# The first loads of a fused condition-and-FFN kernel in runs of 4096 bytes, and what moves with them

## The chip, the cores and the metric

One core of one Trainium2 chip. The metric is the device time of one execution in microseconds, the median of several runs. TensorE (PE) multiplies and transposes, VectorE (DVE), ScalarE (ACT) and GpSimd (POOL) work element by element, SyncE (SP) and ACT issue the transfers (DMA).

## The reference

x has 64 batches of 64 tokens of 512 columns, all float32. A condition q scales it, then comes an FFN with two of six low-rank experts:

```python
q_emb = relu(q @ W3 + b3)
v_sum = sum(v, axis=1, keepdims=True)
x1 = (n * v + v_sum) * q_emb[:, None, :]
y = relu(x1 @ W2 + b2)
base_out = y @ W_base + b_base
shared_out = (y @ A_s) @ B_s
gates = softmax(y @ W_router + b_router)       # two largest kept, others 0: w_per_e
routed_out = sum over e of ((y @ A_r[e]) * w_per_e) @ B_r[e]
out = x + base_out + shared_out + routed_out
```

## The kernel before

The 4096 tokens are worked in eight groups of 512. A group's x lies in `x_nat` by tokens (four tiles t of 128) and, turned, in four chunks c of 128 columns of x with all 512 tokens beside each other. Every product is done in three: each operand is split into a rounded part (`_hi`, made by ACT) and its rest (`_lo`, made by DVE for activations and by POOL for weights), and hi*hi, lo*hi and hi*lo are added up in a PSUM bank. The steps of a group are m1 (x1 times W2, 48 matmuls of 512 columns), h (the experts' first factors), m2 (times W_base) and up (the second factors). Groups 0 to 3 go singly, 4 to 7 in pairs. Each engine runs a program that is written out by hand in one order; semaphores join them, so an instruction that waits holds all behind it on its engine.

The change is about the beginning, group 0. SP issues (L393 to L399) the four tiles of x, the two halves of W3, the four chunks of W2 and W_base. PE first multiplies idle data (`keep_warm`), transposes the condition, then transposes x tile by tile, as each lands, into four banks `head_ps`; tile t stands in columns 128 t to 128 t + 127 of every bank, so the bank's columns are tokens in order and a batch is 64 neighbouring columns. Then it makes q in four chunks (`q`, two halves k of W3 each; float32 operands take two passes each). DVE works on a chunk in the bank itself: `sum_head` (sum per batch, then n times x plus sum), `scale_head` (times q) and, when ACT has rounded (`x1_split_head`), `rest_head`. ACT rounds W2 chunk by chunk (`W2_split`), and POOL makes the rests of W2, then of the router weights and of W_base. `m1_first` on PE consumes chunk 0, then 1, then for output tiles 0 and 1 chunks 2 and 3, then both again for tiles 2 and 3; its waits name the chunk's rounded parts and rests:

```python
for k in range(KC // 2, KC):
    pe.wait_ge(x1_hi_ready, k + 1)
    pe.wait_ge(W2_lo_ready, k + 1)
    for m in tiles:
        chunk(m, k, W2_hi, x_hi)
        chunk(m, k, W2_lo, x_hi)
        pe.wait_ge(x1_lo_ready, k + 1)
        last = chunk(m, k, W2_hi, x_lo)
```

Of the kernel before, what the change touches and what calls it, by code (L numbers as in the profile page):

```python
# [22 lines left out]
def adaln_ffn(nc, x, cond, W3, b3, W2, b2, W_base, b_base, A_s, B_s, A_r, B_r, W_router, b_router, out):  # L23
# [25 lines left out]
    WARM_LOAD, WARM_W3, WARM_HALF, WARM_Q = 8, 1, 2, 1  # L49
# [14 lines left out]
    out_groups = out.rearrange("b n d -> (b n) d").rearrange("(g t p) d -> g p t d", t=TT, p=P)  # L64

    ctx = ExitStack()
    with ctx:
# [79 lines left out]
        hT = bank("hT")  # L147
        q_ps = m1_ps
# [28 lines left out]
        vsum_head_ready = sem("vsum_head_ready")  # L177
# [209 lines left out]
        def _(sp):  # L387
# [22 lines left out]
            def store(g):  # L410

                order = list(up_order[g])
                for t in range(TT):
                    sp.wait_ge(out_ready, TT * g + 1 + max(order.index(i) for i in range(t + 1)))
                    sp.dma_start(out_groups[g][:, t, :], x_nat[g % 2][:, t, :]).then_inc(stored[g % 2], 16)
# [55 lines left out]
        def _(pool):  # L471
# [18 lines left out]
            def scale(g, c):  # L490

                pool.wait_ge(x1_sum_ready, KC * g + c + 1)
                scaled(xs[g % 2][:, c, :], g, c).then_inc(x1_full_ready, 1)
# [149 lines left out]
        def _(act):  # L643
# [8 lines left out]
            def x1_split(g, c):  # L652

                act.wait_ge(x1_full_ready, KC * g + c + 1)
# [24 lines left out]
            def W2_split(c):  # L679

                act.wait_ge(W2_loaded[c], 16)
                nc.scalar.activation(W2_hi[:, c, :], W2_f[:, c, :], ACT.Copy).then_inc(W2_hi_ready, 1)  # L682

            def x1_split_head(c):

                act.wait_ge(x1_full_ready, c + 1)
                nc.scalar.activation(x_hi[:, c, :], head_ps[c][:, :], ACT.Copy).then_inc(x1_hi_ready, 1)  # L687
# [198 lines left out]
        def _(dve):  # L886
# [41 lines left out]

            def sum_head(c):

                dve.wait_ge(head_turned, c + 1)
                nc.vector.tensor_reduce(vsum_head[:, c, :], per_batch(head_ps[c][:, :]), AX.X,
                                        ALU.add).then_inc(vsum_head_ready, 1)
                dve.wait_ge(vsum_head_ready, c + 1)
                nc.vector.scalar_tensor_tensor(
                    out=per_batch(head_ps[c][:, :]), in0=per_batch(head_ps[c][:, :]), scalar=float(N),
                    in1=vsum_head[:, c, :].unsqueeze(2).to_broadcast([P, BG, N]),
                    op0=ALU.mult, op1=ALU.add).then_inc(x1_sum_ready, 1)

            def scale_head(c):  # L940

                dve.wait_ge(qT_ready, c + 1)
                dve.wait_ge(x1_sum_ready, c + 1)
                nc.vector.tensor_tensor(per_batch(head_ps[c][:, :]), per_batch(head_ps[c][:, :]),
                                        qT[:, c, 0:BG].unsqueeze(2).to_broadcast([P, BG, N]),
                                        ALU.mult).then_inc(x1_full_ready, 1)

            def rest_head(c):

                dve.wait_ge(x1_hi_ready, c + 1)  # L950
# [77 lines left out]
            def add_x(g, *places):  # L1028

                for n in places:  # L1030
                    t = up_order[g][n]
                    if g == 0:
                        dve.wait_ge(head_loaded[t], 16)
# [293 lines left out]
        def _(pe):  # L1327
# [9 lines left out]
            nc.tensor.transpose(m1_ps[0][:, 0:B + KC], cond_sb[:, 0:P], ident[0:B + KC, 0:B + KC])  # L1337
            last = nc.tensor.transpose(m1_ps[0][:, cond_cols(1)], cond_sb[0:B, P:2 * P], ident[0:B, 0:B])
            last.then_inc(condT_done, 1)

            for t in range(TT):
                pe.wait_ge(head_loaded[t], 16)
# [15 lines left out]
            def m1(g, m):  # L1358
# [8 lines left out]
                elif m == 0 and g == PAIRED - 1:  # L1367
                    pe.wait_ge(x1_sum_ready, KC * (g + 1))
# [18 lines left out]
            def m1_first():  # L1387

                def chunk(m, k, W, x1):
                    return nc.tensor.matmul(m1_ps[m][:, :], W[:, k, m * P:(m + 1) * P], x1[:, k, :],  # L1390
                                            start=k == 0 and W is W2_hi and x1 is x_hi,
                                            stop=k == KC - 1 and x1 is x_lo)
# [26 lines left out]
                for tiles in ((0, 1), (2, 3)):  # L1419
                    for k in range(KC // 2, KC):  # L1420
                        pe.wait_ge(x1_hi_ready, k + 1)
# [220 lines left out]
```

## Time and profile before

| | us |
|---|---|
| median of 3 runs | 230.55 (230.02 to 230.58) |
| the profiled execution | 230.53 |
| its span in the trace | 228.8 |
| PE busy in the span | 224.0 (98%) |
| DVE busy | 176.1 (77%) |
| ACT busy | 110.2 (48%) |
| POOL busy | 107.0 (47%) |

The profile is one execution. Times in the trace count from the span's start; the 1.7 us between span and execution lie outside it.

### The profile page before, as it was taken

The page shows a single profiled execution, that of the slowest core. Times are in us where ns is not written, and L with a number is a line of the kernel's source. Part 1 is how long each engine was busy: PE and PEld are TensorE (multiplying, and loading weights), DVE is VectorE, ACT ScalarE, POOL GpSimd, SP SyncE. Part 2 cuts the span into 40 slices and gives each one's busy share as a digit, 9 for nine tenths or more (in the row PEclk, how much of TensorE's full clock was granted, in tenths as well). Part 3 has the DMA queues.
Part 4 walks back from the last instruction along what each step waited for, and adds up shares of the span by engine and source line. Part 5 has one row for each costly group of instructions (what it writes and reads, how often), then busy time and mean ns, then how long its engine had stood idle before and what let it go on. Part 6 is the DMA issues. An engine that isn't in the chain of part 4 may idle for free.

```text
span 228.8 us, 2915 instructions
## 1 busy us (share of the span) xinstructions
PE 224.0 (98%) x982; PEld 183.1 (80%) x982; DVE 176.1 (77%) x323; ACT 110.2 (48%) x230; POOL 107.0 (47%) x99
## 2 busy tenths in 40 slices
PE   7999999999999999999999999999999999999994
PEld 3987888888888888888888888888888788888883
DVE  0595979899979979699758899999996969382334
ACT  3178631545426345779326496344676375331010
POOL 4079444058125865889887201349988700000000
PEclk9999999999999999999999999999999999999999
DMA  6999902704049495004429844111213742002044
GB/s 194 324 240 230 276 27 53 165 3 185 10 122 261 181 229 171 15 0 182 181 39 222 150 181 141 48 19 17 82 47 127 287 148 84 0 15 47 27 165 183
DMA packets 32917, 29.05 MB, mean 127 GB/s; under 512 B 5841, under 2 KB 23317, under 8 KB 32902
## 3 DMA queue, kind: packets, MB, share of 16 engines
q1 hardware_dynamic: 31090, 28.69, 44.0%
q10 hardware_dynamic: 1812, 0.17, 0.6%
q8 instruction: 8, 0.13, 0.3%
q14 instruction: 7, 0.06, 0.1%
HBM read 18.89 MB, written 8.39 MB: 119 GB/s over the span
## 4 chain that ended last, share of the span: by engine, by line
PE 94%; DMA 2%; DVE 1%; ACT 1%; SPq 1%; issue 0%; DVEq 0%
PE m_ps L1354 77%; PE hT L1354 11%; PE m_ps L1390 5%; DMA x_nat<-in_x_dram 2%; DVE x_nat L1037 1%; PE m_ps L1382 1%; SPq L394 1%; PE m_ps L1331 0%; PE m_ps L1344 0%; ACT qT L676 0%; ACT W_hi L682 0%; ACT x_hi L687 0%; PE hT L1344 0%; DVEq L1036 0%
## 5 line engine op out<-in xcount | busy, mean ns | idle before, releaser
L487 POOL TENSOR_TENSOR xs<-xs,qT 128x512 f32<-128x512 f32 x22 | 24.1, 1096 | 46.7 <-DVE xs L911 30.8
L1354 PE MATMUL m_ps<-Wb_lo,y_hi 128*128 128x512 f32 x116 | 45.1, 389 | 0.0
L1354 PE MATMUL m_ps<-Wb_hi,y_hi 128*128 128x512 f32 x116 | 45.1, 389 | 0.0
L1354 PE MATMUL m_ps<-Wb_hi,y_lo 128*128 128x512 f32 x116 | 45.1, 389 | 0.0
L659 ACT ACTIVATE y_hi<-m_ps,condT 128x512 fp32r<-128x512 f32 x30 | 20.7, 692 | 17.5 <-PE m_ps L1354 10.0
L1354 PEld LDWEIGHTS m_ps<-Wb_hi,y_hi 128*128 128x128 f32 x116 | 21.8, 188 | 4.5
L1354 PEld LDWEIGHTS m_ps<-Wb_hi,y_lo 128*128 128x128 f32 x116 | 21.8, 188 | 4.5
L1354 PEld LDWEIGHTS m_ps<-Wb_lo,y_hi 128*128 128x128 f32 x116 | 21.8, 188 | 4.5
L926 DVE TENSOR_TENSOR y_lo<-m_ps,y_hi 128x512 fp32r<-128x512 f32 x30 | 20.2, 678 | 5.4 <-ACT m_ps L660 5.4
L1354 PE MATMUL m_ps<-x_hi,W_hi 128*128 128x512 f32 x61 | 23.7, 389 | 0.0
L1354 PE MATMUL m_ps<-x_hi,W_lo 128*128 128x512 f32 x61 | 23.7, 389 | 0.0
L1037 DVE TENSOR_TENSOR x_nat<-m_ps,x_nat 128x512 f32<-128x512 f32 x29 | 18.9, 682 | 4.6 <-PE m_ps L1354 4.6
L1354 PE MATMUL m_ps<-x_lo,W_hi 128*128 128x512 f32 x61 | 21.9, 389 | 0.0
L752 ACT ACTIVATE xs<-xs,offset,q 128x64 f32<-128x64 f32 x48 | 16.6, 431 | 8.3 <-DVE offset L305 6.9
L569 POOL TENSOR_TENSOR x_lo_more<-xs,x_hi_more 128x512 fp32r<-128x512 f32 x12 | 15.4, 1303 | 10.5 <-ACT x_hi_more L743 10.5
L660 ACT ACTIVATE m_ps<-m_ps,condT 128x512 f32<-128x512 f32 x30 | 19.9, 664 | 0.0
L1057 DVE STREAM_TRANSPOSE xs<-x_quart 128x512 f32<-128x512 f32 x16 | 17.4, 1090 | 1.7 <-DMA x_quart<-in_x_dram 1.7
L569 POOL TENSOR_TENSOR x_lo<-xs,x_hi 128x512 fp32r<-128x512 f32 x12 | 15.4, 1294 | 4.0 <-ACT x_hi L743 4.0
L743 ACT ACTIVATE x_hi<-xs 128x512 fp32r<-128x512 f32 x16 | 9.8, 630 | 11.0 <-POOL xs L575 4.0
L655 ACT ACTIVATE x_hi<-xs 128x512 fp32r<-128x512 f32 x12 | 7.6, 635 | 13.4 <-POOL xs L487 13.4
L1354 PEld LDWEIGHTS m_ps<-x_hi,W_hi 128*128 128x128 f32 x61 | 11.4, 188 | 2.4
L1354 PEld LDWEIGHTS m_ps<-x_hi,W_lo 128*128 128x128 f32 x61 | 11.4, 188 | 2.4
(189 smaller groups left out, 494.4 us busy)
## 6 DMA issues: line engine op xcount, KB each, us to landing
out_dram<-x_nat SPq DMA_DIRECT2D x32, 256.0 KB, 2.5
x_quart<-in_x_dram SPq DMA_DIRECT2D x28, 256.0 KB, 4.8
x_nat<-in_x_dram SPq DMA_DIRECT2D x7, 1024.0 KB, 5.5
gatesT<-wT SPq DMA_DIRECT2D x24, 48.0 KB
x_nat<-in_x_dram SPq DMA_DIRECT2D x4, 256.0 KB, 4.0
W_f<-in_L_cond_W_dram SPq DMA_DIRECT2D x4, 256.0 KB, 6.2
Wb_f<-in_L_ffn_W_base_dram SPq DMA_DIRECT2D x1, 1024.0 KB, 8.8
W_sb<-in_L_cond_W_dram SPq DMA_DIRECT2D x2, 256.0 KB, 5.4
```

What stands on the lines that cost most here:

```text
L487: return nc.gpsimd.tensor_tensor(per_batch(tile), per_batch(tile), qT[:, c, BG * g:BG * (g + 1)].unsqueeze(2).to_broadcast([P, BG, N]), AL ...
L569: nc.gpsimd.tensor_tensor(lo_of(name, kk), tile_of(name, kk), hi_of(name, kk).bitcast(F32), ALU.subtract).then_inc(pair_lo_ready, 1)
L655: nc.scalar.activation(x_hi[:, KC * (g % 2) + c, :], xs[g % 2][:, c, :], ACT.Copy).then_inc(x1_hi_ready, 1)
L659: nc.scalar.activation(y_hi[:, g % 2, m, :], ps[:, :], ACT.Relu, bias=b2_sb[:, m:m + 1]).then_inc(y_hi_ready, 1)
L660: nc.scalar.activation(ps[:, :], ps[:, :], ACT.Relu, bias=b2_sb[:, m:m + 1]).then_inc(y_full_ready, 1)
L743: nc.scalar.activation(hi_of(name, kk), tile_of(name, kk), ACT.Copy).then_inc(pair_hi_ready, 1)
L752: nc.scalar.activation(xs[half][:, c, toks], xs[half][:, c, toks], ACT.Identity, bias=offset[:, n - 1, b:b + 1], scale=q64[:, c, which:whi ...
L926: nc.vector.tensor_tensor(y_lo[:, g % 2, m, :], ps[:, :], y_hi[:, g % 2, m, :].bitcast(F32), ALU.subtract).then_inc(y_lo_ready, 1)
L1037: nc.vector.tensor_tensor(x_nat[g % 2][:, t, :], m2_of[g][t][:, :], x_nat[g % 2][:, t, :], ALU.add).then_inc(out_ready, 1)
L1057: nc.vector.transpose(xs[half][:, c, :], x_quart[half][:, :, :].rearrange("p b (i c) -> p c b i", c=KC)[:, c]).then_inc(pair_turned, 1)
L1354: mm = nc.tensor.matmul(psum, lhsT, rhs, start=start and i == 0, stop=stop and i == len(terms) - 1)
L1390: return nc.tensor.matmul(m1_ps[m][:, :], W[:, k, m * P:(m + 1) * P], x1[:, k, :], start=k == 0 and W is W2_hi and x1 is x_hi, stop=k == K ...
```

## The change

The first x is loaded so that a partition holds four neighbouring tokens (4p to 4p + 3), two per load, in runs of 4096 bytes; W3 (rows 2p and 2p + 1) and W2 are loaded in runs of 4096 bytes too. Where W3 takes rows 2p + k, the condition's columns are transposed with a stride of 2. Column 128 t + p of a bank now is token 4p + t, so the 64 tokens of a batch lie in four strides of 16 columns: the sum is taken over two axes, and add and scale are four instructions of 128 columns each. q is made chunk by chunk, with one idle matmul fewer. The head's chunks go in the order 0, 1, 3, 2; chunk 3's sum is written to SBUF (`x_third`, a part of `xs[0]`), and POOL scales it there. In group 1 DVE's first sum is split around another rest.

```diff
-            for t in range(TT):
-                sp.dma_start(x_nat[0][:, t, :], x_groups[0][:, t, :]).then_inc(head_loaded[t], 16)
-            for k in range(QC):
-                sp.dma_start(W3_sb[:, k, :], W3[k * P:(k + 1) * P, :]).then_inc(W3_loaded[k], 16)
-            for c in range(KC):
-                sp.dma_start(W2_f[:, c, :], W2.rearrange("(p c) n -> p c n", c=KC)[:, c, :]).then_inc(W2_loaded[c], 16)
+            for i in range(2):
+                sp.dma_start(x_nat[0][:, 2 * i:2 * i + 2, :], x_head[:, 2 * i:2 * i + 2, :]).then_inc(head_loaded[i], 16)
+            sp.dma_start(W3_sb[:, :, :], W3.rearrange("(p k) n -> p k n", k=QC)).then_inc(W3_loaded, 16)
+            for i in range(2):
+                sp.dma_start(W2_f[:, 2 * i:2 * i + 2, :],
+                             W2.rearrange("(p c) n -> p c n", c=KC)[:, 2 * i:2 * i + 2, :]).then_inc(W2_loaded[i], 16)
...
-            for c in range(KC):
-                pool.wait_ge(W2_hi_ready, c + 1)
+            for n, c in enumerate(HEAD_ORDER):
+                if n == 2:
+                    pool.wait_ge(qT_ready, KC)
+                    pool.wait_ge(head_sum_ready, 3 * TT)
+                    third = x_third.rearrange("p (t b i) -> p t b i", t=TT, b=BG)
+                    for t in range(TT):
+                        nc.gpsimd.tensor_tensor(third[:, t], third[:, t], qT[:, KC - 1, 0:BG].unsqueeze(2).to_broadcast(
+                            [P, BG, N // TT]), ALU.mult).then_inc(x_third_ready, 1)
+                pool.wait_ge(W2_hi_ready, n + 1)
                 W_rest(W2_lo[:, c, :], W2_f[:, c, :], W2_hi[:, c, :], W2_lo_ready)
...
             q_relu(0)
             q_relu(1)
             W2_split(0)
+            x1_split_head(0)
             q_relu(2)
-            x1_split_head(0)
             q_relu(3)
             x1_split_head(1)
             W2_split(1)
+            W2_split(3)
             W2_split(2)
-            x1_split_head(2)
-            W2_split(3)
+            x1_split_head(3)
             act.wait_ge(Wd_loaded, 16 * (2 + KC))
             nc.scalar.activation(Wd_hi[:, :, :], Wd_f[:, :, :], ACT.Copy).then_inc(Wd_hi_ready, 1)
-            x1_split_head(3)
+            x1_split_head(2)
...
+            def add_head(c):
+
+                dve.wait_ge(vsum_head_ready, HEAD_ORDER.index(c) + 1)
+                for t in range(TT):
+                    nc.vector.scalar_tensor_tensor(
+                        out=by_batch(x_third if c == KC - 1 else head_ps[c][:, :])[:, t], in0=by_batch(head_ps[c][:, :])[:, t],
+                        scalar=float(N), in1=vsum_head[:, c, :].unsqueeze(2).to_broadcast([P, BG, N // TT]),
+                        op0=ALU.mult, op1=ALU.add).then_inc(head_sum_ready, 1)
...
+                for t in range(TT):
+                    nc.vector.tensor_tensor(by_batch(head_ps[c][:, :])[:, t], by_batch(head_ps[c][:, :])[:, t],
+                                            qT[:, c, 0:BG].unsqueeze(2).to_broadcast([P, BG, N // TT]),
+                                            ALU.mult).then_inc(head_full_ready, 1)
...
-                nc.vector.tensor_tensor(x_lo[:, c, :], head_ps[c][:, :],
+                dve.wait_ge(x1_hi_ready, HEAD_ORDER.index(c) + 1)
+                nc.vector.tensor_tensor(x_lo[:, c, :], x_third if c == KC - 1 else head_ps[c][:, :],
                                         x_hi[:, c, :].bitcast(F32), ALU.subtract).then_inc(x1_lo_ready, 1)
...
             y_rest_single(0, 1)
-            total(1, 0)
+            sum_x(1, 0)
             y_rest_single(0, 2)
+            y_rest_single(0, 3)
+            add_sum(1, 0)
             turn_x(1, 1)
-            y_rest_single(0, 3)
             total(1, 1)
...
-            for k in range(QC):
-                pe.wait_ge(W3_loaded[k], 16)
-                for c in range(KC - 1):
+            pe.wait_ge(W3_loaded, 16)
+            for c in range(2):
+                for k in range(QC):
                     q(k, c)
-                keep_warm(WARM_HALF if k == 0 else WARM_Q)
-            for k in range(QC):
-                q(k, KC - 1)
+            keep_warm(WARM_Q)
+            for c in range(2, KC):
+                for k in range(QC):
+                    q(k, c)
```

DVE, group 0, from the first rest on. Before (`m_ps` is a PSUM bank, `hT` the bank of chunk 3):

```order
L951 TENSOR_TENSOR x_lo<-m_ps,x_hi 128x512
L932 TENSOR_REDUCE vsum_head<-m_ps 128x8
L935 SCALAR_TENSOR_TENSOR m_ps<-m_ps,vsum_head 128x512
L944 TENSOR_TENSOR m_ps<-m_ps,qT 128x512
L951 TENSOR_TENSOR x_lo<-m_ps,x_hi 128x512
L932 TENSOR_REDUCE vsum_head<-hT 128x8
L935 SCALAR_TENSOR_TENSOR hT<-hT,vsum_head 128x512
L944 TENSOR_TENSOR hT<-hT,qT 128x512
```

The same stretch of DVE after the change (`xs` is `x_third`, in SBUF):

```order
L978 TENSOR_TENSOR x_lo<-m_ps,x_hi 128x512
L954 TENSOR_REDUCE vsum_head<-hT 128x8
L961 SCALAR_TENSOR_TENSOR xs<-hT,vsum_head 128x128 x4
L978 TENSOR_TENSOR x_lo<-m_ps,x_hi 128x512
L954 TENSOR_REDUCE vsum_head<-m_ps 128x8
L961 SCALAR_TENSOR_TENSOR m_ps<-m_ps,vsum_head 128x128 x4
L971 TENSOR_TENSOR m_ps<-m_ps,qT 128x128 x4
L978 TENSOR_TENSOR x_lo<-xs,x_hi 128x512
L978 TENSOR_TENSOR x_lo<-m_ps,x_hi 128x512
```

Chunk 3 (bank `hT`) now comes ahead of chunk 2, it has no scale on DVE, and its rest reads `xs` and `x_hi`.

POOL, from the end of its memsets on. Before (`W_lo` are the rests of W2):

```order
L483 MEMSET gatesT 32x512
L504 TENSOR_TENSOR W_lo<-W_f,W_hi 128x512 x4
L504 TENSOR_TENSOR Wd_lo<-Wd_f,Wd_hi 128x512
L504 TENSOR_TENSOR Wb_lo<-Wb_f,Wb_hi 128x512 x4
L487 TENSOR_TENSOR xs<-xs,qT 128x512 x2
```

After:

```order
L490 MEMSET gatesT 32x512
L511 TENSOR_TENSOR W_lo<-W_f,W_hi 128x512 x2
L519 TENSOR_TENSOR xs<-xs,qT 128x128 x4
L511 TENSOR_TENSOR W_lo<-W_f,W_hi 128x512 x2
L511 TENSOR_TENSOR Wd_lo<-Wd_f,Wd_hi 128x512
L511 TENSOR_TENSOR Wb_lo<-Wb_f,Wb_hi 128x512 x4
```

The four pieces of chunk 3's scale stand between the second and the third rest of W2, and everything behind them on POOL comes after them.

PE, from the first q to m1. Before (`idle` is the filler):

```order
L1382 MATMUL m_ps<-condT,W_sb 128x64 x3
L1331 MATMUL m_ps<-idle 128x512 x2
L1382 MATMUL m_ps<-condT,W_sb 128x64 x3
L1331 MATMUL m_ps<-idle 128x512
L1382 MATMUL m_ps<-condT,W_sb 128x64 x2
L1390 MATMUL m_ps<-x_hi,W_hi 128x512 x3
```

After:

```order
L1378 MATMUL hT<-ident,x_nat 128x128
L1362 MATMUL m_ps<-idle 128x512
L1416 MATMUL m_ps<-condT,W_sb 128x64 x4
L1362 MATMUL m_ps<-idle 128x512 x2
L1416 MATMUL m_ps<-condT,W_sb 128x64 x4
L1424 MATMUL m_ps<-x_hi,W_hi 128x512 x3
```

The first four q are now both halves of chunks 0 and 1, and one idle matmul has gone; the order of m1's matmuls stays, with chunks 3 and 2 exchanged.

## Rows read from the trace of the kernel before

**Rows 1.** The page: the chain that ended last, shares by engine.

```profile
PE 94%; DMA 2%; DVE 1%; ACT 1%; SPq 1%; issue 0%; DVEq 0%
```

**Rows 2.** The same chain in order of time: start us, us, what.

```profile
2.18 5.16 DMA x_nat<-in_x_dram
...
7.39 0.63 PE m_ps L1344 x3
8.02 0.12 PE hT L1344
...
8.35 1.36 PE m_ps L1382 x6
...
12.53 11.46 PE m_ps L1390 x48
```

**Rows 3.** Timeline of PE: start us, us, line, what; two passes to a q.

```profile
9.98 1.40 PE L1382 MATMUL m_ps<-condT,W_sb 128*128 128x64 f32 x6
...
18.71 0.50 PE L1390 MATMUL m_ps<-x_lo,W_hi 128*128 128x512 f32 x1
...
19.74 0.39 PE L1390 MATMUL m_ps<-x_hi,W_hi 128*128 128x512 f32 x1
```

**Rows 4.** Waits of 0 to 30 us: us in total, times, longest.

```profile
PEld m_ps L1390 <- DVE x_lo L951: 0.4, 1, 0.4
```

**Rows 5.** Landing of the first x piece (last number, us); windows: last three clock, DMA share, GB/s.

```profile
x_nat<-in_x_dram SPq DMA_DIRECT2D x1, 256.0 KB, 2.5
...
3.00:4.00 1.00, 1.00 (x4) 0.40 (x3) 0.00 (x0) 0.99 (x2) 0.14 (x1) 1.00 1.02 335
...
11.00:12.00 1.00, 1.00 (x7) 1.00 (x7) 1.00 (x2) 1.00 (x4) 0.13 (x1) 1.00 1.11 393
```

**Rows 6.** Timeline of DVE, group 0: the first sum, then chunk 2 and a rest.

```profile
7.81 0.69 DVE L932 TENSOR_REDUCE vsum_head<-m_ps 128x8 f32<-128x512 f32 x1 [6.61 <-PE m_ps L1344]
...
13.12 0.68 DVE L932 TENSOR_REDUCE vsum_head<-m_ps 128x8 f32<-128x512 f32 x1
13.83 0.70 DVE L935 SCALAR_TENSOR_TENSOR m_ps<-m_ps,vsum_head 128x512 f32<-128x512 f32 x1
14.64 0.70 DVE L944 TENSOR_TENSOR m_ps<-m_ps,qT 128x512 f32<-128x512 f32 x1
15.25 0.68 DVE L951 TENSOR_TENSOR x_lo<-m_ps,x_hi 128x512 fp32r<-128x512 f32 x1
```

**Rows 7.** Timeline of DVE: two short operations without a wait between them.

```profile
30.91 0.18 DVE L978 TENSOR_TENSOR logit<-m_ps,lmax 128x24 f32<-128x24 f32 x1
31.01 0.18 DVE L979 TENSOR_TENSOR m_ps<-m_ps,lmax 128x24 f32<-128x24 f32 x1
```

**Rows 8.** Timeline of ACT: x_hi of chunk 1, then two W2 chunks.

```profile
12.62 0.59 ACT L687 ACTIVATE x_hi<-m_ps 128x512 fp32r<-128x512 f32 x1
13.10 1.15 ACT L682 ACTIVATE W_hi<-W_f 128x512 fp32r<-128x512 f32 x2
```

**Rows 9.** Timeline of POOL: a pair of rests, a scale, a short product.

```profile
13.81 2.54 POOL L504 TENSOR_TENSOR W_lo<-W_f,W_hi 128x512 fp32r<-128x512 f32 x2 [0.66 <-ACT W_hi L682]
...
29.22 1.04 POOL L487 TENSOR_TENSOR xs<-xs,qT 128x512 f32<-128x512 f32 x1 [2.46 <-DVE xs L911]
...
160.33 0.22 POOL L305 TENSOR_TENSOR offset<-vsum_pair,qT 128x8 f32<-128x8 f32 x1
```

**Rows 10.** Timelines of DVE and POOL where DVE reads two SBUF operands.

```profile
118.79 1.29 POOL L582 TENSOR_TENSOR xs<-xs 128x512 f32<-128x512 f32 x1
119.41 1.22 DVE L1091 TENSOR_TENSOR x_lo<-xs,x_hi 128x512 fp32r<-128x512 f32 x1 [2.37 <-ACT x_hi L743]
120.04 1.75 POOL L588 TENSOR_TENSOR xs<-xs 128x512 f32<-128x512 f32 x1
...
167.15 2.53 POOL L569 TENSOR_TENSOR x_lo<-xs,x_hi 128x512 fp32r<-128x512 f32 x2
168.45 1.79 DVE L1078 SCALAR_TENSOR_TENSOR xs<-xs,vsum_pair 128x512 f32<-128x512 f32 x1
```

More of the change, by code:

```diff
@@ L47, in adaln_ffn @@
     RO = 32
-    WARM_LOAD, WARM_W3, WARM_HALF, WARM_Q = 8, 1, 2, 1
+    WARM_LOAD, WARM_W3, WARM_Q = 8, 1, 2
     PAIRED = 4
@@ L64, in adaln_ffn @@
     out_groups = out.rearrange("b n d -> (b n) d").rearrange("(g t p) d -> g p t d", t=TT, p=P)
+    x_head = x.rearrange("b n d -> (b n) d")[0:TG, :].rearrange("(p t) d -> p t d", t=TT)
+    out_head = out.rearrange("b n d -> (b n) d")[0:TG, :].rearrange("(p t) d -> p t d", t=TT)
     ctx = ExitStack()
@@ L147, in adaln_ffn @@
         hT = bank("hT")
+        x_third = xs[0][:, KC - 1, :]
+        HEAD_ORDER = (0, 1, 3, 2)
         q_ps = m1_ps
@@ L414, in store @@
                     sp.wait_ge(out_ready, TT * g + 1 + max(order.index(i) for i in range(t + 1)))
-                    sp.dma_start(out_groups[g][:, t, :], x_nat[g % 2][:, t, :]).then_inc(stored[g % 2], 16)
+                    rows = out_head if g == 0 else out_groups[g]
+                    sp.dma_start(rows[:, t, :], x_nat[g % 2][:, t, :]).then_inc(stored[g % 2], 16)
             def load_x(g):
@@ L679, in W2_split @@
             def W2_split(c):
-                act.wait_ge(W2_loaded[c], 16)
+                act.wait_ge(W2_loaded[c // 2], 16)
                 nc.scalar.activation(W2_hi[:, c, :], W2_f[:, c, :], ACT.Copy).then_inc(W2_hi_ready, 1)
             def x1_split_head(c):
-                act.wait_ge(x1_full_ready, c + 1)
-                nc.scalar.activation(x_hi[:, c, :], head_ps[c][:, :], ACT.Copy).then_inc(x1_hi_ready, 1)
+                if c == KC - 1:
+                    act.wait_ge(x_third_ready, TT)
+                else:
+                    act.wait_ge(head_full_ready, TT * (c + 1))
+                nc.scalar.activation(x_hi[:, c, :], x_third if c == KC - 1 else head_ps[c][:, :],
+                                     ACT.Copy).then_inc(x1_hi_ready, 1)
             q_relu(0)
@@ L935, in sum_head @@
[L935 to L938, printed above, removed]
+                nc.vector.tensor_reduce(vsum_head[:, c, :], by_batch(head_ps[c][:, :]).rearrange("p t b i -> p b t i"),
+                                        AX.XY, ALU.add).then_inc(vsum_head_ready, 1)
@@ L1336, in _ @@
             pe.wait_ge(cond_loaded, 32)
[L1337 to L1338 removed]
+            nc.tensor.transpose(m1_ps[0][:, B:B + KC], cond_sb[B:B + KC, 0:P], ident[B:B + KC, B:B + KC])
+            for k in range(QC):
+                last = nc.tensor.transpose(m1_ps[0][:, cond_cols(k)],
+                                           cond_sb[0:B, :].rearrange("p (f k) -> p k f", k=QC)[:, k], ident[0:B, 0:B])
             last.then_inc(condT_done, 1)
             for t in range(TT):
[L1342 removed]
+                if t % 2 == 0:
+                    pe.wait_ge(head_loaded[t // 2], 16)
                 for c in range(KC):
@@ L1391, in chunk @@
                                             start=k == 0 and W is W2_hi and x1 is x_hi,
-                                            stop=k == KC - 1 and x1 is x_lo)
+                                            stop=k == HEAD_ORDER[-1] and x1 is x_lo)
                 pe.wait_ge(x1_hi_ready, 1)
@@ L1419, in m1_first @@
                 for tiles in ((0, 1), (2, 3)):
-                    for k in range(KC // 2, KC):
-                        pe.wait_ge(x1_hi_ready, k + 1)
-                        pe.wait_ge(W2_lo_ready, k + 1)
+                    for n, k in enumerate(HEAD_ORDER[KC // 2:], KC // 2):
+                        pe.wait_ge(x1_hi_ready, n + 1)
+                        pe.wait_ge(W2_lo_ready, n + 1)
                         for m in tiles:
```

45 lines of the change are left out of this document (22 added, 23 removed).

## The prediction

> **What bounds the kernel now.** I read the chain that ended last first: 94% of it is PE [rows 1]. In order of time, only its head is anything else: the fourth 256 KB piece of the first group's x is issued at 2.18 us and lands at 7.34, PE transposes it from 7.39, and from 12.53 an unbroken 11.46 us of m1 products of group 0 follows, and behind it matmuls to the end [rows 2]. There are 48 of them, 0.23 us apart when PE doesn't wait; from 18.71 to 19.74 are four, 0.33 behind a wait and then 0.23 or 0.24 [rows 3]. The list of waits of the first 30 us has one PE wait inside m1, 0.4 us of the weight loader on x_lo (0.14 us of it reaches the matmuls: 18.71 instead of about 18.57) [rows 3, 4]. So the time moves by what this beginning moves, one for one: I compare one slot, the matmul at **19.74**, the first on the last chunk of group 0. 18 of the 48 follow from there on, and the list has no PE wait behind it, so what shifts the slot shifts the end.
>
> The profiled execution spans 228.8 us and took 230.53, which is 0.02 from the median of 230.55; I add the shift of the slot to 230.53.
>
> **The loads.** SP issues two x loads for four, one W3 load for two, two W2 loads for four, each in runs of 4096 bytes for 2048; the bytes stay. An issue costs SP about 0.45 us, but issue does not set the landing: the first x piece lands 2.5 us after its issue, the fourth 5.16 us after [rows 2, 5]. What sets it is the rate: 335 GB/s in the microsecond from 3.00, 393 GB/s from 11.00 with the same engines [rows 5]. No row shows a 4096-byte run. Bound above: no gain, the second half of x lands at L = 7.34 as now. Bound below: 3.31 for the first piece and three more of 262 KB at 393 GB/s, 0.67 each, L = 5.3. I take half the step from 335 to 393 GB/s, 7% of the 5.16 us, **L = 7.0**, near the upper bound, since the moved bytes are the same and the late piece was late while the engines were all busy. The Trainium skill (DMA: Bandwidth & Descriptors, Specifications) puts line rate at transfers of 512 B and up, so by it 2048-byte runs had nothing left to give. By that rule L would be 7.34 and everything below 0.34 later.
>
> **PE up to m1.** Behind the late landing stand eight transposes instead of four; one more costs 0.12 (8.02 to 8.14 [rows 2]), so 4 x 0.12 = 0.48 us. That is the first loss. DVE's first sum started at 7.81, 0.47 after the landing [rows 2, 6]; now T = L + 0.47 + 0.48 = L + 0.95 = **7.95**, 0.14 later than before. The q passes follow at L + 1.5 = 8.5 (before: 8.35 [rows 2]) with one filler (8.14 to 8.35, 0.21 [rows 2]) fewer. They go chunk by chunk now, so the first chunk's sum needs four passes at 0.23 (six took 1.40 [rows 3]), 0.93, and is done at 9.4; with some 0.6 for its relu, q is there by 10.1. m1 could start near 12.2 for 12.53: a gain of 0.3 at the front, if the rest kept up.
>
> **DVE.** Before, a unit is sum, 0.71, add, 0.81, scale, 0.61, next [rows 6]. Now add and scale are four pieces of 128 columns. A piece: two 24-column operations with no wait between them stand 0.10 apart [rows 7], 512 columns 0.61, hence 0.00105 us a column and 0.21 for 128. Four pieces are 0.84 for 0.61; where the next operation needs their result, 3 x 0.21 + 0.30 + 0.11 = 1.04 for 0.81. From T: sum 0 at 0, add 0.71, sum 1 at 1.55, scale 0 at 2.16 (10.1, q is there), add 1 at 3.00, scale 1 at 4.04, rest 0 at 4.88, sum 3 at 5.49, add 3 at 6.20, rest 1 at 7.04, sum 2 at 7.65, add 2 at 8.36, scale 2 at 9.40, and **rest 3 asks at T + 10.24** = 18.19. One scale is POOL's now, and DVE has no wait left in this stretch; the pieces use up both.
>
> **POOL and ACT.** POOL now scales chunk 3 between the second and third W2 rest. Scale 1 ends at T + 4.97; x_hi(1) starts 0.03 later, W_hi(1) 0.48 after it and lasts 0.63 [rows 8]; POOL starts W_lo(1) 0.08 later, T + 6.19, and a rest has a pitch of 1.25 and lasts 1.29 [rows 9]: the pieces begin at T + 7.44. Price q of a piece: below, the scale form, 1.04 for 512 columns against 0.22 for 8 gives 0.41 less 0.04 of overlap, 0.37; above, the plain form, 1.29, gives 0.43 [rows 9]. I take **0.41**, toward the upper, since I take the repeated operand for what makes the scale form cheap, and it now repeats over 16 columns instead of 64. So W_lo(3) runs from T + 9.08 to T + 10.37, and PE may begin chunk 3 at T + 10.42 = 18.37; without it PE would be there near 17.8. ACT fits between (x_hi(3) starts at T + 9.1).
>
> **The shared resource.** Rest 3 now reads x_third and x_hi, both in SBUF; every rest of the head before read a PSUM bank and ran 0.68 beside POOL's 13.81 to 16.35 [rows 6, 9]. Where DVE reads two SBUF operands while POOL works, the trace shows it held: asked at 119.41 during POOL's 118.79 to 120.08, it ended at 120.63, 0.55 after POOL's end, and POOL's next, put out at 120.04, stretched to 1.75 and ended 1.16 after DVE's end; asked at 168.45, just after POOL's second operation of a pair had started, it took 1.79 and ended 0.55 after that one [rows 10]. Who asks first wins. Here DVE asks at T + 10.24 and POOL puts out W_lo(2) at T + 7.44 + 4q + 1.25 = T + 8.69 + 4q: with q over **0.39** DVE is ahead. With 0.41 (T + 10.33): rest 3 ends at T + 10.92, PE takes x_lo(3) at T + 10.97 = 18.92, W_lo(2) ends at T + 10.92 + 1.16 = T + 12.08, and the slot, four matmuls on (1.03), waits for it: T + 12.13 = **20.08**. The Trainium skill (SBUF — State Buffer, Who interferes with whom) says the same: a DVE instruction with two SBUF inputs contends with a GpSimd one that reads SBUF, and issue order decides who blocks. The trace agrees, with 1.22 and 1.79 us for 0.68.
>
> **The rest** I cost at nothing. The third transpose of cond and its strided reads lie ahead of the x landing, for which PE waits. Group 1's sum is split and one rest moved ahead of it on DVE, in a stretch where no wait of PE is listed [rows 4]; if that cover went, it would cost up to one rest, 0.6. POOL ends Wd_lo near T + 13.3 = 21.3 and the first Wb_lo near 22.5, and PE reads both from 24.0 on, when m1 ends [rows 2]; 1.5 us of that cover would have to go before it costs anything.
>
> **Sum.** 20.08 - 19.74 = +0.34: 230.53 + 0.34 = **230.9 us**. In terms: transposes +0.48, loads -0.34, and the chain from T to the slot 12.13 for 11.93, +0.20. What the front gives is not kept, since POOL and DVE end later than PE would.
>
> **Rivals.**
> 1. *POOL wins the port* (slower). It decides from q = 0.39 down; with DVE's pieces at 0.22, 13 of which stand between, from 0.42 down. At q = 0.37: W_lo(2) runs from T + 10.17 to T + 11.46, rest 3 ends at T + 12.01, PE has it at T + 12.06 = 20.01, and the slot is at 21.04: +1.30, **231.8 us**. For it: the 0.05 us between the two; against it: that short runs hardly cost the least price. 0.30.
> 2. *The loads come much sooner* (faster). If the late share of x was late only for the number of packets, L goes to 5.3 to 5.9; at 5.6 the slot is T + 12.13 = 6.55 + 12.13 = 18.68, -1.06, **229.5 us**. For it: the first piece needed 2.5 us and the fourth 5.16; against it: the engines were busy all that time. It passes the 0.3% from L = 5.97. 0.20.
> 3. *The loads don't gain*, the bytes being the same. L = 7.34, else as forecast: +0.68, **231.2 us**; for it, that the engines were busy throughout; it is the upper end of my case and has 0.15 of its chance.
>
> **How the numbers follow.** My case has 0.50, and with L from 6.6 to 7.34 its own range is 230.5 to 231.2. What a measurement here can tell from no change is 0.3%, 0.69 us: below 229.86 faster, above 231.24 slower. Faster: rival 2's 0.20 less the part above 229.86, 0.16. Slower: 0.26 of rival 1 (its rest has an early L) and 0.10 of my case (late L with q above 0.43, or a part I priced at nothing), 0.36. Same: 0.48. The range goes from 229.9 (inside rival 2, about 0.12 below it) to 231.9 (rival 1 with a late L, some 0.08, above it).
>
> **What the profile after would show.** The landing of the second x load (7.0; its window of DMA rate over 335 GB/s); first sum at 7.95; pieces 0.21 apart on DVE and 0.41 on POOL; the rest on SBUF at 18.2, ending 0.55 behind a POOL operation, and behind which of the two; a PE wait on POOL's W_lo of about 0.5 and the slot at 20.1. I would be wrong if L is under 6, if the lock falls to POOL, or if the longer gap of PE before the second landing lowers the granted clock, which was 1.00 in both microseconds shown [rows 5].

## The result, and the profile after

The changed kernel took 232.87 us (median of 4 runs, 232.28 to 233.08) beside 230.56 us for the kernel before (230.02 to 230.63, 4 runs): ratio 1.0104, 95% interval 1.0088 to 1.012. That is 2.3 us slower, and above the range of the prediction. The profiled execution took 232.94 us with a span of 231.2.

The page of the changed kernel gives the chain that ended last by engine; it answers to [rows 1]:

```profile
PE 90%; DVE 3%; DMA 2%; POOL 2%; issue 1%; ACT 0%; ACTq 0%; DVEq 0%
```

The same chain in order of time (start us, us, what), which answers to [rows 2]:

```profile
1.39 4.98 DMA cond_sb<-in_L_cond_b_dram
...
7.17 0.84 PE m_ps L1378 x3
8.23 0.64 PE m_ps L1378 x3
9.08 0.64 PE m_ps L1378 x3
10.07 0.70 DVE vsum_head L954
10.79 0.89 DVE m_ps L961 x4
...
16.09 0.93 POOL W_lo L511
17.35 1.48 POOL xs L519 x4
18.83 1.26 POOL W_lo L511
20.23 1.72 PE m_ps L1424 x6
21.98 4.36 PE m_ps L1424 x18
```

The chain no longer begins with the last piece of x. It begins with the load of b2's rows into `cond_sb`, 2 KB on ACT's queue, which lands at 6.37 us. x is not late: by the DMA events its halves land at 5.08 and 6.68 us, where the fourth piece landed at 7.34 before [rows 2]. Nor is the condition itself the last (64 KB, whole at 5.43 us, 3.56 before): PE waits for the 2 KB. PE's timeline at this place, of the kernel before (first fence) and of the changed one (second):

```profile
2.52 2.34 PE L1331 MATMUL m_ps<-idle 128*128 128x512 bf16 x5
4.65 0.32 PE L1337 MATMUL m_ps<-ident,cond_sb 68*128 68x68 f32 x1
...
6.08 0.51 PE L1344 MATMUL m_ps<-ident,x_nat 128*128 128x128 f32 x3
6.43 0.28 PE L1344 MATMUL hT<-ident,x_nat 128*128 128x128 f32 x1
6.55 0.60 PE L1344 MATMUL m_ps<-ident,x_nat 128*128 128x128 f32 x3
```

```profile
3.37 1.49 PE L1362 MATMUL m_ps<-idle 128*128 128x512 bf16 x3
6.50 0.24 PE L1368 MATMUL m_ps<-ident,cond_sb 4*128 4x4 f32 x1 [1.65 <-DMA cond_sb<-in_L_cond_b_dram]
...
8.03 0.84 PE L1378 MATMUL m_ps<-ident,x_nat 128*128 128x128 f32 x3
8.66 0.42 PE L1378 MATMUL hT<-ident,x_nat 128*128 128x128 f32 x1
8.88 0.84 PE L1378 MATMUL m_ps<-ident,x_nat 128*128 128x128 f32 x3
```

Two things went wrong. The condition's transposes, behind which all transposes of x stand on PE, start at 6.50 instead of 4.65, after 1.65 us in which PE idled. And the transposes of x are 0.21 us apart instead of 0.12: 8.03 to 8.88 for four, where before 6.08 to 6.55. The granted clock has its first record at 9.77 us here (6.02 before), at full speed; the pitch falls to 0.12 with it. So the first sum, my T, is at 10.07 instead of 7.81 [rows 6], 2.26 us later.

From T on nearly all is as forecast. The timelines of DVE and POOL at the end of the chain:

```profile
18.79 3.04 POOL L511 TENSOR_TENSOR W_lo<-W_f,W_hi 128x512 fp32r<-128x512 f32 x2
19.20 0.89 DVE L971 TENSOR_TENSOR m_ps<-m_ps,qT 128x128 f32<-128x128 f32 x4
20.00 0.68 DVE L978 TENSOR_TENSOR x_lo<-xs,x_hi 128x512 fp32r<-128x512 f32 x1
20.23 0.47 PE L1424 MATMUL m_ps<-x_hi,W_hi 128*128 128x512 f32 x1 [0.27 <-POOL W_lo L511]
...
21.98 0.47 PE L1424 MATMUL m_ps<-x_hi,W_hi 128*128 128x512 f32 x1
```

DVE asked for rest 3 at 20.00, T + 9.93 (forecast T + 10.24), and POOL put out the second of its pair, W_lo(2), at 20.04, so DVE was first by 0.04 us, ran its 0.68, and the pair took 3.04 us where an undisturbed one took 2.54 [rows 9]. The slot, the first matmul on the last chunk of group 0, is at 21.98, T + 11.91. Before it was T + 11.93.

### The profile page after: what moved, and what is told of

It reads as the page before. It is cut to its first block, busy times and chain, and to the rows that moved or that the text cites. A ratio compares the mean times of both kernels' runs of the same rounds, so it can differ in the third digit from the quotient of the medians.

```text
span 231.2 us, 2934 instructions
## 1 busy us (share of the span) xinstructions
PE 224.8 (97%) x982; PEld 183.6 (79%) x982; DVE 176.7 (76%) x343; ACT 110.4 (48%) x230; POOL 108.9 (47%) x103
## 4 chain that ended last, share of the span: by engine, by line
PE 90%; DVE 3%; DMA 2%; POOL 2%; issue 1%; ACT 0%; ACTq 0%; DVEq 0%
PE m_ps L1388 76%; PE hT L1388 11%; PE m_ps L1424 3%; DMA cond_sb<-in_L_cond_b_dram 2%; DVE x_nat L1067 1%; PE m_ps L1378 1%; POOL W_lo L511 1%; DVE m_ps L971 1%; DVE m_ps L961 1%; POOL xs L519 1%; DVE vsum_head L954 0%; PE hT L1378 0%; ACT x_hi L704 0%; ACTq L658 0%; ACT W_hi L696 0%
```

## The experiments

**Theory A**: PE's late start, and the low clock behind it, are the loss; the cause is the load ahead of the condition's. **Theory B**: the loss is in the pieces on DVE and POOL and in their shared access to SBUF. T is the start of DVE's first sum, a filler is an idle matmul, and times in brackets stand for the kernel before in the same runs. In all 16 profiles the time from the slot to the end of the execution is 210.8 to 211.3 us, so what sets one profiled execution apart from another lies ahead of the slot, to within 0.5 us.

**e2_warm12: the clock alone.** Four more fillers bridge PE's idle stretch; nothing else changes.

```diff
-    WARM_LOAD, WARM_W3, WARM_Q = 8, 1, 2
+    WARM_LOAD, WARM_W3, WARM_Q = 12, 1, 2
```

> The changed kernel with 12 idle matmuls at the start for 8: PE waits as long for the condition, but isn't idle from 4.86 us on. It separates the two parts of theory A. If the wait alone costs, nothing changes (232.9). If the level of the clock costs, the sixteen transposes of x stand 0.12 us apart instead of 0.21, the first sum comes at about 8.9 to 9.1 instead of 10.06, and the time is 231.8 to 232.0. Theory B expects 232.9.

Measured: 231.75 us (230.15), ratio 1.0074 (1.0052 to 1.0096). PE's timeline, with the condition's transpose where it was in the changed kernel and the pitch of x's back at 0.12 (7.55 + 0.48 = 8.03):

```profile
6.49 0.27 PE L1368 MATMUL m_ps<-ident,cond_sb 4*128 4x4 f32 x1
...
7.55 0.28 PE L1378 MATMUL hT<-ident,x_nat 128*128 128x128 f32 x1
...
8.03 0.28 PE L1378 MATMUL hT<-ident,x_nat 128*128 128x128 f32 x1
```

T is 8.95 (10.07 in the changed kernel) and the slot 20.85, T + 11.91, as expected. Of the 2.24 us that the changed kernel's slot lay behind, the clock was 1.13, and 1.11 is left with the late start. By the medians, each against the kernel before in its own runs, the share of the clock is smaller: 1.6 us are left of 2.3.

**e7_cond_mid: start and clock.** The condition's three transposes stand between x's first and second half, so that PE begins with what has landed.

```diff
-            pe.wait_ge(cond_loaded, 32)
-            (the condition's three transposes)
             for t in range(TT):
+                if t == TT // 2:
+                    pe.wait_ge(cond_loaded, 32)
+                    (the condition's three transposes)
```

> The changed kernel with the condition's transposes between those of the first and the second half of x, when the condition has just landed (6.4 us), so that the copy of the condition is ready by the time of the first q. Theory A expects the first sum at about 8.0 and, if the granted clock holds, 230.3 to 230.8 us; where it falls to its lower level between 8 and 12 us, as in the run with the condition last, up to 2 us more.

Measured: 231.48 us (230.33), ratio 1.0046 (1.0028 to 1.0065). In the profile, of an execution of 230.89 us, x's transposes start at 5.26, the granted clock is up from 5.69 to the end, T is 7.96 and the slot 19.88, 0.14 behind before's. The chain, which begins with x again:

```profile
0.81 4.32 DMA x_nat<-in_x_dram
```

Of the changed kernel's 2.3 us this takes back 1.2 in the medians, less than expected. The six executions split by their mean granted clock: 230.89 and 230.99 us at 1.0, and 231.36 to 231.73 at 0.999 to 0.993. **e8_cond_mid_fill** (the same with WARM_LOAD 9, WARM_W3 2, WARM_Q 4) was to hold the clock.

> As the run before, with four more idle matmuls (one more at the start, one more ahead of q, two more between the q chunks), 0.22 us each at the full level, some 0.7 us on PE's way to m1. If it is PE's thin work between x and m1 that lets the clock fall, it holds here in all executions, and the time is 230.6 to 231.0, with less scatter than the run without them; if fillers do nothing to the clock, it is as much slower as they take.

Measured: 231.78 us (230.33), ratio 1.0061 (1.0042 to 1.008); T 7.91, slot 20.25. The fillers stand on PE's path here and gain nothing, so this expectation missed too. Nor do these executions split by the clock: 231.09 and 231.93 us both have 1.0. That the clock makes e7's slower executions is therefore not shown.

**e14_before_warm5: the clock alone, in the kernel before.** Fewer fillers; PE starts the condition's transposes when it did.

```diff
-    WARM_LOAD, WARM_W3, WARM_HALF, WARM_Q = 8, 1, 2, 1
+    WARM_LOAD, WARM_W3, WARM_HALF, WARM_Q = 5, 1, 2, 1
```

> The kernel before with five fillers for eight ahead of the condition's transposes: PE idles about 1.3 us longer before them and starts them when it did (4.65 us); loads and orders unchanged. If the late clock costs by itself: it rises near 8 us instead of 6.02, x's last transposes and the first q passes run at half pace, the first sum is near 8.2 and the slot 0.5 to 1.2 later: 231.0 to 231.8 us. If only PE's late start costs: 230.2 to 230.8 us.

Measured: 231.52 us (231.36 to 231.73; before 230.4), ratio 1.0053 (1.0034 to 1.0073). PE's timeline:

```profile
4.70 0.35 PE L1337 MATMUL m_ps<-ident,cond_sb 68*128 68x68 f32 x1 [1.13 <-DMA cond_sb<-in_L_cond_b_dram]
...
6.20 0.84 PE L1344 MATMUL m_ps<-ident,x_nat 128*128 128x128 f32 x3
...
7.06 0.84 PE L1344 MATMUL m_ps<-ident,x_nat 128*128 128x128 f32 x3
...
9.19 1.41 PE L1382 MATMUL m_ps<-condT,W_sb 128*128 128x64 f32 x6
```

The start is the same (4.70 for 4.65) and x lands no later, but the pitch is 0.21 and q begins at 9.19 instead of 8.19: slot 20.63, +0.88. All 16 transposes of x take 3.4 us at this level and bind; at the upper one PE waits for x between them. The granted clock has its first record at 9.37. So the expectation held, slot and time.

**e13_before_gate4 and e12_before_gate: the start alone, in the kernel before.** One more wait ahead of PE's first transposes, for the fourth and for the third piece of x.

```diff
+            pe.wait_ge(head_loaded[TT - 1], 16)     # e12: head_loaded[TT // 2]
             pe.wait_ge(cond_loaded, 32)
```

> The kernel before, all its loads, orders and operations unchanged, with one more wait ahead of PE's first transposes: for the third 256 KB piece of x (6.47 us in the profile of before, about when the condition lands in the changed kernel). Theory A (PE's late start alone makes the changed kernel slower, whatever its runs and pieces): the fillers end at 4.9, PE idles till 6.5, the clock comes up late and the x transposes run 0.21 us apart, the first sum of DVE is at 9.7 to 10.1 instead of 7.81 and the slot follows by as much less what slack lies between: 232.0 to 232.8 us. Theory B (the new chain of DVE and POOL has a share in it): the chain of before from T to the slot has slack, as where W2 came in two loads (0.82 us of an earlier T gave 0.16 us of slot), and takes up most of the delay: 230.6 to 231.6 us.

> The kernel before with PE's first transposes behind a wait for the fourth piece of x (7.34 us in the profile of before). PE idles from 4.9 us to about 7.3. Theory A with the clock: the granted clock comes up at 10 us or later, the 18 transposes run 0.21 us apart and the first sum of DVE is near 11.3: all executions slow, 232.8 to 234 us. Theory A without it (idle time only): the clock is up before 7.3, transposes 0.12 apart, first sum near 9.9: 231.5 to 232.3 us. If before's chain has slack enough for a late start: under 231.2 us.

e13 measured 233.85 us (233.65 to 234.2; before 230.4), ratio 1.0154 (1.0135 to 1.0172): slower than the changed kernel, with every load, run and operation of before. Timeline of PE and two windows (the last three columns: granted clock, DMA share, GB/s):

```profile
7.04 0.25 PE L1338 MATMUL m_ps<-ident,cond_sb 68*128 68x68 f32 x1 [2.36 <-DMA x_nat<-in_x_dram]
```

```profile
6.00:7.00 1.00, 0.00 (x0) 0.00 (x0) 0.00 (x0) 0.00 (x0) 0.00 (x0) 1.00 1.02 336
...
8.00:9.00 1.00, 1.00 (x6) 1.00 (x5) 0.00 (x0) 0.00 (x0) 0.00 (x0) 0.50 0.89 193
```

Here the record shows what the pitch told elsewhere: behind an idle stretch of 2.36 us the granted clock falls to 0.50 at 7.80 (1.2 GHz of the two levels 1.2 and 2.4), the transposes are 0.21 us apart, and it is back at 11.22. T is 10.33, the slot 22.59. The expectation with the clock held.

e12 measured 232.16 us (230.46), ratio 1.0059 (1.003 to 1.0087), but its 12 executions form two groups: five from 230.22 to 230.80 and seven from 232.11 to 234.41. The profile is of the fastest: the third piece had landed at 5.27, PE waited only 0.5, the clock was up from 4.71. In it T is 7.63 and the slot 19.43. The slower group has no profile; that it is e13's case is argued from e13, not seen.

**e6_before_x2: the large transfer alone.** The kernel before with x in two 512 KB loads, in its own rows and 2048-byte runs.

```diff
-            for t in range(TT):
-                sp.dma_start(x_nat[0][:, t, :], x_groups[0][:, t, :]).then_inc(head_loaded[t], 16)
+            for i in range(2):
+                sp.dma_start(x_nat[0][:, 2 * i:2 * i + 2, :], x_groups[0][:, 2 * i:2 * i + 2, :]).then_inc(head_loaded[i], 16)
```

> The kernel before with one part done alone: the first x in two transfers of 512 KB, in the old layout and with runs of 2048 bytes. Theory A expects the condition near 6.4 us, PE idle in between, the first sum at 9.5 to 10 instead of 7.81, and 231.8 to 232.6 us. Theory B expects the time of before, 230.1 to 230.6; so does a theory by which only the length of the runs delays the condition.

Measured: 231.21 us (230.33), ratio 1.0035 (1.0008 to 1.0062), again in two groups: 230.00 to 230.65 (four) and 231.77 to 232.26 (four). The profile, of the first group, has the condition's loads at 4.83 and T at 7.81, so there a 512 KB load ahead made no late start. The other four have the time that was expected, but no profile: whether their condition came late is not shown.

**e4_x_split and e5_x_four: 256 KB loads in the changed kernel.** e4 cuts each x load by partitions (64 and 64, runs of 4096 bytes), e5 by rows (four loads, runs of 2048 bytes).

```diff
+                for u in range(2):
+                    part = slice(64 * u, 64 * u + 64)
+                    sp.dma_start(x_nat[0][part, 2 * i:2 * i + 2, :], x_head[part, 2 * i:2 * i + 2, :]).then_inc(head_loaded[i], 16)
```

> The changed kernel with each of its two x loads cut in two by partitions (64 each): runs of 4096 bytes as in the changed kernel, but 256 KB a load as before. It asks what held up the condition's loads. If it is the size of the first load in front of them, the condition lands near 4.3 us again and the time is 230.5 to 231.2; if it is the length of the runs, it lands at about 6.4 and the time stays at 232.9.

> The changed kernel with one part undone: x is loaded in four transfers of 256 KB with runs of 2048 bytes, in the new layout (tokens 4p + t); all else stays, the four-piece operations and W3 and W2 in runs of 4096 bytes too. Theory A (a 512 KB transfer put out ahead of the condition's holds that back, PE starts late and slow) expects the condition at about 4.3 us, the first sum near 7.8, and 230.2 to 230.9 us. Theory B (pieces and POOL) expects 232.9.

The condition landed at 4.49 in e4 and 5.00 in e5, for 6.37: runs of 4096 bytes in a load of 256 KB don't hold it. Nor did 512 KB in runs of 2048 bytes in e6's profile (4.83); every profile with both together shows 6.25 to 6.43 us. The time went the other way: 234.45 us (230.15), ratio 1.017 (1.0117 to 1.0222), and 233.77 us (230.33), ratio 1.0138 (1.0102 to 1.0174). (e4's profile is of its one execution at 232.18; the other three took 234.30 to 234.83, so what it shows is the better case.) x's last part now landed at 7.97 and 8.77 us, for 6.68, and the clock, up at 4.90 and 4.78, fell again: in e4 from 8.32 to 11.73, amid x's transposes and q, in e5 from 11.60 to 18.43, amid q and the first part of m1. Two windows of e5:

```profile
10.00:11.00 1.00, 0.83 (x4) 0.86 (x4) 1.00 (x5) 0.00 (x0) 0.00 (x0) 1.00 1.05 397
...
14.00:15.00 1.00, 1.00 (x5) 1.00 (x5) 1.00 (x5) 0.38 (x2) 0.49 (x1) 0.50 1.02 119
```

Ahead of this fall the engine had idled 1.47 us for x's last piece and 0.39 for W3. My expectation for both missed, since it took the landing of x as given. Why x's last part is this late I can't say; e11 (below) had W2's merged loads behind x and no such delay, and W3's merged load alone was in no run.

**e1_cond_late and e3_cond_first: two more orders.** e1 has the condition's transposes behind x's sixteen, e3 the condition's two loads on SP's queue ahead of x.

```diff
+            sp.dma_start(cond_sb[0:B, :], cond).then_inc(cond_loaded, 16)
+            sp.dma_start(cond_sb[B:B + KC, 0:P], b2.rearrange("(k p) -> k p", p=P)).then_inc(cond_loaded, 16)
-            act.dma_start(cond_sb[0:B, :], cond).then_inc(cond_loaded, 16)
-            act.dma_start(cond_sb[B:B + KC, 0:P], b2.rearrange("(k p) -> k p", p=P)).then_inc(cond_loaded, 16)
```

> The changed kernel, with PE's three transposes of the condition moved behind the sixteen of x, so that PE no longer waits first for the condition's loads (landed at 6.37 us in the changed kernel, 4.26 before). Theory A (the late start of PE: it waits for the condition, goes idle at 4.86, and transposes at the slow level till 9.7) expects the second half of x at about 6.7 us to be what PE waits for, the first sum on DVE near 7.6 to 8.0 instead of 10.06, and 230.4 to 231.0 us. Theory B (the four-piece operations on DVE and the shared operands with POOL are what costs) expects no more than 0.4 us less than the changed kernel's 232.9.

> The changed kernel with the condition's and b2's loads issued by SP ahead of x instead of by ACT beside it. Theory A: the condition has landed before 4.5 us, PE goes over from the idle matmuls without a gap, x lands about 1 us later than in the changed kernel (7.5 to 7.9), the first sum comes at about 8.7, and the time is 231.3 to 231.8. Theory B expects 232.9 or, with the later x, 233.5.

Measured: e1 232.82 us, ratio 1.0114 (1.0073 to 1.0155); e3 232.57 us, ratio 1.0108 (1.0077 to 1.014), both beside 230.15. In e1 the start is right (T 7.64, 0.17 sooner than before), but the clock fell from 11.46 to 18.29, through the first 12 of m1's 48 matmuls, which are then 0.43 us apart for 0.23, and the slot came at 22.36. e3 has the condition by 3.04, but SP's x loads follow two issues later (second half 7.55, T 8.50), and the clock fell from 12.38 to 15.79. In both, what PE did before the fall was q's passes of 64 columns and, ahead of them, transposes with an idle stretch among them (0.29 us for x's second half in e1). That this made the fall is not shown: e11's q passes come right behind an idle stretch of 0.44 us, and its clock held. One gain was paid for with another slow stretch, and both expectations missed the time.

**e9_mid_early: who asks first.** e7 with one line moved on ACT, so that POOL comes to W_lo(2) sooner.

```diff
             q_relu(2)
+            W2_split(1)
             q_relu(3)
             x1_split_head(1)
-            W2_split(1)
```

> The version with the condition's transposes between x's halves (231.48 us), with one line moved on ACT: the second W2 split stands ahead of the fourth relu of q instead of behind the second x_hi. POOL then starts its second W2 rest at 12.43 instead of 13.98 us and the four pieces of x_third at 14.9 (when DVE's third add is done) instead of 15.25. Theory P (who asks first has the port): POOL's third W2 rest is then put out near 16.35 and the fourth near 17.6, ahead of DVE's rest of chunk 3, which asks at 17.84; that rest is held to 0.55 us behind the POOL operation, ends near 19.4, the last rest near 20.1, and the slot moves from 19.88 to about 20.2: 231.7 to 231.9 us. Theory Q (the 0.42 and 0.22 us for which PE waits for POOL are simply lost time of POOL): the slot comes 0.3 earlier, 231.1 to 231.2 us.

Measured: 231.71 us (230.58), ratio 1.0052 (1.0032 to 1.0072), clock at 1.0 in nine of twelve executions. Timelines of POOL, DVE and PE:

```profile
16.66 2.53 POOL L511 TENSOR_TENSOR W_lo<-W_f,W_hi 128x512 fp32r<-128x512 f32 x2
...
18.10 1.64 DVE L978 TENSOR_TENSOR x_lo<-xs,x_hi 128x512 fp32r<-128x512 f32 x1
19.16 1.75 POOL L511 TENSOR_TENSOR Wd_lo<-Wd_f,Wd_hi 128x512 fp32r<-128x512 f32 x1
...
19.80 0.50 PE L1425 MATMUL m_ps<-x_lo,W_hi 128*128 128x512 f32 x1 [0.99 <-DVE x_lo L978]
```

This is my rival 1. POOL's second W rest is put out near 17.9, before DVE asks at 18.10; DVE is held, ends at 19.74, 0.55 behind POOL's 19.19, and PE waits 0.99. The slot is 20.84, T + 12.67 for T + 11.92 in e7. So an earlier POOL costs 0.75 us from T to the slot in these profiles (theory P; Q falls), more than the 0.3 that I expected of it. The medians show less, 231.71 for 231.48 us, and beside the kernel before in their own runs no difference (1.13 and 1.15); e7's median stands on six executions, four of them slower for a reason that I did not find.

**e10_mid_whole: the price of the pieces.** e7 with DVE's add and scale as one operation of 512 columns each; it sums and scales the first group's tokens by the wrong batches, so its values there are not the reference's, while its order of work is e7's.

> The same version with add and scale of DVE as one operation of 512 columns each instead of four of 128. With the rows in four strides one operation can't take the batches as they stand, so this kernel adds and scales the wrong 64 columns together: the first group's values are not the reference's, the shapes and the order of the work are. Theory C (the pieces cost DVE what I said, 0.23 us for each of seven operations): DVE asks for the rest of chunk 3 at T + 9.0 instead of T + 9.93, but it needs x_hi(3) from POOL's four pieces (about 17.2 us) and then stands behind POOL's W2 rest till 17.9; the slot comes 0.2 to 0.3 earlier, at 19.6 to 19.7: 231.1 to 231.3 us. Theory A (what is left over before is the clock and the late landings, the pieces lie beside other work): within 0.15 of 231.48 us. If DVE's pieces bound the chain from T alone, the slot would come 0.9 earlier: 230.6 us.

Measured: 230.96 us (230.58), ratio 1.0021 (0.9998 to 1.0044). That fits none of the three: it is 0.5 us under e7, or 0.8 by each one's distance to the kernel before (0.38 for 1.15). The profile, of an execution of 231.26 us, has T at 8.28 and the slot at 20.22, T + 11.94:

```profile
17.80 1.11 DVE L976 TENSOR_TENSOR x_lo<-xs,x_hi 128x512 fp32r<-128x512 f32 x1 [0.50 <-ACT x_hi L704]
```

DVE came 0.9 sooner to rest 3, then waited 0.50 for x_hi(3) and stood behind POOL (1.11 for 0.68). But this is an execution with late loads (x whole at 7.33 and W3 at 8.60, for 6.63 and 7.93 in e7): the last relu of q came at T + 4.68 for T + 4.42, x_hi(1) behind it 0.69 after its scale was done, and POOL began its second rest at T + 6.08 for T + 6.03. So the profile shows no cost of the pieces between T and the slot, but is a poor place to look for one; by the medians they may cost 0.5 to 0.8 us. A share of theory B is left open there.

**e11_before_w2: W2's half of the change alone**, in the kernel before: two loads of 512 KB in runs of 4096 bytes.

```diff
-            for c in range(KC):
-                sp.dma_start(W2_f[:, c, :], ...[:, c, :]).then_inc(W2_loaded[c], 16)
+            for i in range(2):
+                sp.dma_start(W2_f[:, 2 * i:2 * i + 2, :], ...[:, 2 * i:2 * i + 2, :]).then_inc(W2_loaded[i], 16)
```

> The kernel before with W2 in two loads of 512 KB (4096-byte runs) instead of four of 256 KB, x and W3 as before. If the merged loads behind x take rate from x's last piece (as the last of four x pieces landed at 8.77 us when W3 and W2 were merged behind it), x's last piece lands later than 7.34 us, the first sum of DVE moves with it, and the time is 230.9 to 231.6 us. If only loads ahead of the condition's matter (theory A), the condition lands at 4.3, the last x piece near 7.3, the second W2 half near 10.4, and the time stays at 230.1 to 230.6 us.

Measured: 230.5 us (230.58), ratio 0.9986 (0.9965 to 1.0007): no change, as theory A expected. W2's large loads behind x did no harm. By chance the profile has x's fourth piece at 6.36 and T at 7.00, 0.81 sooner than before, and the slot at 19.59, only 0.16 sooner. PE is the bound there, with its q passes and fillers from 7.97 to m1 at 12.38, and what held q was W3:

```profile
7.97 1.59 PE L1383 MATMUL m_ps<-condT,W_sb 128*128 128x64 f32 x6 [0.44 <-DMA W_sb<-in_L_cond_W_dram]
```

## Why the prediction was wrong

**The step that failed** is the one I cost at nothing: "The third transpose of cond and its strided reads lie ahead of the x landing, for which PE waits." The order is right, the cover is not. I looked at when x lands and not at when the condition does. Its two loads are on ACT's queue, issued at 0.82 and 1.39 us (1.41 before). The last to land is the 2 KB of b2; SP had begun to issue two x loads ahead of it, of 256 KB each before and of 512 KB now. It came in together with the second of them: at 4.22 to 4.27 us beside 4.04 to 4.40 before, at 6.29 to 6.37 beside 6.04 to 6.68 now. It isn't bound to it, since in the profiles of e4 (4.49) and e6 (4.83) it was there sooner: in the profiles it took 512 KB and runs of 4096 bytes together to hold it. How it is held (which of the 16 engines, in what order) no row tells.

The first wait on PE is for these two loads, so all 16 transposes went behind, not the eight that I charged with 0.48 us. The slot came 2.24 us late: by e2, 1.11 of it is the late start and 1.13 the low clock behind the idle stretch. e13 (start and clock, slot +2.85) and e14 (clock alone, +0.88) make such losses in the kernel before, whose loads and operations stay as they are. In e7's profile PE neither starts late nor stays at the low clock, and the slot is 0.14 behind before's.

**The clock** I named as what could make me wrong, and gave it no price and no chance. The reason was a column that reads 1.00 in both microseconds shown [rows 5], though its first record comes only at 6.02. The pitch in PE's rows was there to read: 0.21 us a transpose ahead of that record, 0.12 behind it.

**L, the landing of x,** was forecast at 7.0 and was 6.68. But five executions with the four x loads of before had the last one at 6.36 (e11), 6.42 (e12), 6.80 (e14), 6.95 (e13) and 7.34 (before), and seven with the new two had the second at 6.54 to 6.78, once at 7.33 (e10). The middle ones are 6.80 and 6.68: my -0.34 us was a difference to one sample, the latest of five, and rival 3 (no gain) was near the truth. (A slip beside it: half the step from 335 to 393 GB/s is 8% of the time, not 7, and gives L = 6.93.) The bytes did move faster, 387, 358 and 386 GB/s in the three microseconds from 4.00 for 224, 318 and 338 in the profile of before; what came clearly sooner was W2, behind x on the queue, whole at 10.41 to 11.21 us in those seven for 11.55 to 12.14 with the loads of before (before, e6, e12 to e14).

**"Moves one for one"** holds for the new chain (T + 11.91 to 11.94 in after, e2, e7 and e10) and not for the old (T + 11.80 in e12, T + 12.59 in e11), where PE binds when x is early. Rival 2 priced an early x without W3: q's passes need it, and it landed at 7.96 in the changed kernel, where an L of 5.6 would have them start at L + 1.5 = 7.1. What an L of 5.6 would have gained no run shows.

**From T to the slot** the sum came out right, 11.91 for 12.13, and the order at the port partly by luck. DVE's pieces were 0.20 apart for 0.21, POOL's 0.36 for 0.41. By my own rule a piece under 0.39 gives POOL the port; it did not, because DVE asked 0.31 us sooner than I had it, and two errors of like size left it ahead by 0.04 us for my 0.09. Rival 1 did not occur, but e9 shows that it is real: the slot at T + 12.67 in that order, where I had priced T + 13.09. The W_lo waits of PE (0.43 at 19.57 and 0.20 at 21.55) ate the gain at the front of m1, as the sum said. The rest of group 1, Wd_lo and Wb_lo cost PE no wait.

**What stays open:** e7 has T and clock as before, and its profiled execution, at 230.89 us, is 0.36 above before's: 0.14 of that is the slot, the other 0.22 is within what the stretch behind the slot scatters. But its median is 1.15 above the kernel before in the same runs; its slower executions have no profile, and by e10 the pieces may have a share. Nor is it settled why x's last part came so late in e4 and e5. No version beat the kernel before.

## What to carry to other kernels

When small and large transfers share the DMA engines, ask of each landing what is ahead of it on every queue: making the x loads larger and their runs longer delayed a 2 KB load of another queue by 2 us, and that was what PE waited for first. An engine's first wait sets its start; look at the whole list of what it needs, not only at the latest to land. And where PE idles near the start, price the low level of the clock from the pitch of like instructions in the rows, since the clock column may not have begun; then give it a chance of its own. A landing read in one execution is a sample, and a profile whose loads come late can hide what an experiment was to show.

## What the runs showed that I had not expected

- A load of 64 KB and one of 2 KB on ACT's queue, issued at 0.82 and at 1.39 to 1.41 us in every case, had both landed at 4.27, 4.55, 4.57, 4.59, 4.61 and 5.00 us behind x in loads of 256 KB and runs of 2048 bytes (before, e12, e14, e13, e11, e5), at 4.49 with those of e4, at 6.25 to 6.43 behind 512 KB in runs of 4096 bytes (after, e1, e2, e7 to e10), and at 4.83 behind 512 KB in runs of 2048 bytes (e6).
- The granted clock is nothing that one fixes in one place: e1, e3, e4 and e5 each had it up sooner than the changed kernel (4.63 to 5.55 us for 9.77) and each had it fall once more, for 3.4 to 6.8 us, before or in m1.
- The Trainium skill (SBUF — State Buffer, Who interferes with whom) has issue order decide between DVE and GpSimd; after (DVE first by 0.04 us) and e9 (POOL first by 0.2) agree, and a DVE operation that was held ended 0.55 us behind a POOL operation in e9 and e10 as in [rows 10].
